# Bucket pass of a two-layer graph network: the order of sums and picks on TensorE, one-hot rows on ScalarE, index loads without bounds checks

## The reference

```python
Wh = h @ W + b
row, col = (edge_index[0], edge_index[1])     # src, dst
sc = softplus(deg_coeff[0] * deg_v + deg_coeff[1])
Wr, Wc = Wh[row], Wh[col]
dot = sum(Wr * Wc, axis=-1)
sim = dot / maximum(sqrt(sum(Wr * Wr)) * sqrt(sum(Wc * Wc)), EPS)
base = adj_v * sc * (row != col)
prop_pos = segment_sum((base * relu(sim))[:, None] * Wc, row)
prop_neg = segment_sum((base * -relu(-sim))[:, None] * Wc, row)
out = scale * (coeff[0] * prop_pos + coeff[1] * prop_neg + coeff[2] * Wh)
```

## Time and profile before

| | |
|---|---|
| median of 3 runs | 9028.44 us (9014.64 to 9034.27) |
| the profiled execution | 9029.22 us |
| its span, first to last instruction | 9027.7 us |
| mean granted TensorE clock | 0.755 |
| busy: PE, DVE | 5872.2, 4667.3 us (65%, 52%) |
| busy: ACT, POOL | 2507.0, 5394.6 us (28%, 60%) |

### The profile page before, as it was taken

One profiled execution on the slowest core, in us unless ns is written; L12 is line 12 of the kernel. 1 busy time (PEld: TensorE's weight loads), 2 busy tenths in 40 slices (PEclk: granted clock), 3 DMA queues, 4 the chain that ended last, 5 costly groups with the idle time before them and its releaser, 6 DMA issues. The chain is left out here.

```text
span 9027.7 us, 97916 instructions
## 1 busy us (share of the span) xinstructions
PE 5872.2 (65%) x22770; PEld 3836.2 (42%) x22771; DVE 4667.3 (52%) x8116; ACT 2507.0 (28%) x4153; POOL 5394.6 (60%) x5308
## 2 busy tenths in 40 slices
PE   0088888888705787777772354444444478888886
PEld 0044444444402444444441232222222268888886
DVE  2645555555433444444443454444444467777777
ACT  0044444444402444444441122222221211111111
POOL 5777777777667777777776477777777710000000
PEclk9988888888856888888886566666666667777776
DMA  9344444444423333333331122222222111111111
GB/s 340 95 127 128 132 127 132 127 132 126 137 67 84 102 102 102 101 101 103 102 101 41 41 66 64 63 63 63 64 63 63 56 45 40 41 40 39 40 41 35
DMA packets 561626, 798.11 MB, mean 88 GB/s; under 512 B 162586, under 2 KB 306858, under 8 KB 553354
## 3 DMA queue, kind: packets, MB, share of 16 engines
q1 hardware_dynamic: 371912, 482.15, 17.6%
q0 software_dynamic: 172640, 195.75, 10.3%
q10 hardware_dynamic: 16994, 119.45, 3.2%
HBM read 497.93 MB, written 298.87 MB: 88 GB/s over the span
## 5 line engine op out<-in xcount | busy, mean ns | idle before, releaser
L691 POOL DMA_INDIRECT rows_by_src_bucket<-arena,put_idx x1568 | 1604.2, 1023 | 493.9 <-issue 443.5
L623 POOL DMA_INDIRECT G<-h_rows,src_idx x1568 | 1542.6, 984 | 477.8 <-issue 477.5
L623 POOL DMA_INDIRECT G<-in_x,src_idx x1470 | 1557.3, 1059 | 448.0 <-issue 435.1
L743 PE MATMUL ps_gv<-arena,w_src 128*128 128x512 f32 x1568 | 1013.6, 783 | 0.0
L805 PE MATMUL ps_pos<-arena 128*128 128x392 f32 x390 | 325.3, 937 | 1047.4 <-DVE arena L1171 1047.4
L740 PE MATMUL ps_gv<-attr,w_attr 65*128 65x512 f32 x1568 | 1000.8, 773 | 0.0
L1209 DVE TENSOR_SCALAR arena<-ps_gv 128x512 f32<-128x512 f32 x392 | 266.7, 680 | 1279.4 <-PE ps_gv L746 1279.0
L733 PE MATMUL ps_two<-ident,G 128*128 128x128 f32 x1568 | 303.1, 326 | 762.5 <-DMA G<-h_rows,src_idx 428.1
L1150 DVE TENSOR_TENSOR_SCAN xd_t<-same,xd_t,ps_two 128x512 f32<-128x512 bf16 x588 | 749.6, 1275 | 88.6 <-PE ps_two L722 46.1
L722 PE MATMUL ps_two<-ident,inj 128*128 128x128 f32 x2352 | 399.2, 298 | 606.9 <-DMA inj<-first_edge_rows 606.9
L919 ACT COPY arena<-ps_out 128x512 f32<-128x512 f32 x392 | 229.7, 586 | 2004.9 <-PE ps_out L753 2004.9
(11 more groups left out here) (221 smaller groups left out, 10040.4 us busy)
## 6 DMA issues: line engine op xcount, KB each, us to landing
inj<-first_edge_rows SPq DMA_DIRECT2D x588, 256.0 KB, 3.0
running_sums<-arena SPq DMA_DIRECT2D x392, 256.0 KB
same<-same_dst SPq DMA_DIRECT2D x1176, 64.0 KB, 2.6
rows_by_src_bucket<-zeros ACTq DMA_DIRECT2D x62, 1072.0 KB
first_edge_rows<-zeros ACTq DMA_DIRECT2D x56, 896.0 KB, 5.8
attr<-in_attr_t SPq DMA_DIRECT2D x392, 128.0 KB, 3.6
G<-h_rows,src_idx POOLq DMA_INDIRECT x1568
rows_by_src_bucket<-arena,put_idx POOLq DMA_INDIRECT x1568, 2.3
```

The lines of the kernel that those rows point to most:

```text
L623: pool.indirect_dma_start(out_, None, table_in, bass.IndirectOffsetOnAxis(ap=index, axis=0)).then_inc(s, 16)
L691: pool.indirect_dma_start(bucket_d, bass.IndirectOffsetOnAxis(ap=put_idx[:, buf, k:k + 1], axis=0), put[:, buf, k], None).then_inc(s_added ...
L743: pe.matmul(ps_gv[:, buf % 2, k], w_src[:, layer, k], xs_t[:, buf % 2], start=False, stop=False)
```

## The change

There are three parts, and one line of set-up that goes with the second.

- On TensorE the arguments of `pipeline` are exchanged: sums of n-1 first, then picks of n, then marks of n+2.
- The one-hot rows are made by ScalarE (`make_marks`) and no longer by VectorE: the absolute value of lane minus row, with the negated row number as a per-partition bias, eight times 128x128, and then relu(1 - that) over all 1024 columns in place. The row numbers are negated where they are first computed.
- The bounds checks of the index loads on TensorE and VectorE are left out. The loads stay.

```diff
@@ pick, TensorE
-                        min_val=0, max_val=(NT - 1) * (D + 1))[1]
+                        min_val=0, max_val=(NT - 1) * (D + 1),
+                        skip_runtime_bounds_check_because="a count of bucket ends, at most NT - 1")[1]
...
@@ TensorE
-            pipeline(pe, (pick, 0), (sum_unit, 1), (turn_marks, -2), n=NU, trips=UTRIPS)
+            pipeline(pe, (sum_unit, 1), (pick, 0), (turn_marks, -2), n=NU, trips=UTRIPS)
@@ ScalarE
+            def make_marks(h, buf):
+                act.wait_ge(s_unit[buf], h * 16 + 16)
+                act.wait_ge(s_outs, udone(h, buf, NB))
+                row_now = rows[buf].rearrange("p a (j f) -> p (a j) f", f=RW)[:, :, ROW_AT]
+                for k in range(SLOTS):
+                    away = nc.scalar.activation(onehot[:, buf % NB, k], lane[:], ACT.Abs, bias=row_now[:, k:k + 1])
+                steps.then(away)
+                both = onehot[:, buf % NB].rearrange("p k e -> p (k e)")
+                nc.scalar.activation(both, both, ACT.Relu, bias=1.0, scale=-1.0).then_inc(s_onehot, 1)
...
+            steps.begin()
+            for buf in range(3):
+                make_marks(0, buf)
+            steps.end()
             copy_marks(0, 0)
-            pipeline(act, (copy_marks, -1), (roots, 0), n=NU, trips=UTRIPS)
+            pipeline(act, (copy_marks, -1), (roots, 0), (make_marks, -3), steps=steps, per=NU, n=NU, trips=UTRIPS)
@@ VectorE, set-up
-            then(v.tensor_scalar(row_of[:], deg_tmp, 0.0, None, ALU.add))
+            then(v.tensor_scalar(row_of[:], deg_tmp, -1.0, None, ALU.mult))
@@ VectorE, bucket pass
-            def mark_rows(h, buf):
-                dve.wait_ge(s_unit[buf], h * 16 + 16)
-                dve.wait_ge(s_outs, udone(h, buf, NB))
-                row_now = rows[buf].rearrange("p a (j f) -> p (a j) f", f=RW)[:, :, ROW_AT]
-                v.tensor_tensor(onehot[:, buf % NB], across(lane[:], SLOTS), along(row_now, P),
-                                ALU.is_equal).then_inc(s_onehot, 1)
...
-                        max_val=(NT - 1) * D)[1]
+                        max_val=(NT - 1) * D,
+                        skip_runtime_bounds_check_because="a count of bucket ends, at most NT - 1")[1]
...
-            for buf in range(3):
-                mark_rows(0, buf)
-            pipeline(dve, (weigh, 0), (add_unit, 2), (mark_rows, -3), steps=steps, per=8 * NU, n=NU, trips=UTRIPS)
+            pipeline(dve, (weigh, 0), (add_unit, 2), steps=steps, per=8 * NU, n=NU, trips=UTRIPS)
```

## The result

The changed kernel takes 10,147 us (median; 10,144 to 10,152) against 9,025 in runs of the kernel before on the same chip: ratio 1.1245, 95% interval 1.1225 to 1.1264. It is slower by an eighth, as forecast (10,080 in a range of 9,640 to 10,200). The profiled execution has a span of 10,150.7 us and took 10,152.3.

A forecast was written before the change was run, and what follows sets the result against it. TensorE, nearly full in the bucket pass at mixed clock, and VectorE at the high level bound the kernel. The new serial loop takes 11.05 us for 6.81: 247 periods give +1047, start +6, over 9029.2: 10,080 us, range 9,990 to 10,200.

The forecast's parts named there:

- The loop: Bucket pass: picks, weigh, add, sums, next picks run serially, 11.33 us a unit at the low clock, 7.98 at the high.
- The clock: TensorE's clock in the bucket pass: low in bursts, rising at their end; one twelfth of burst time high, 11.05 us a unit.
- all low: Edge case of the bucket pass with the clock never high in the bursts: 10,151 us.
- The earlier trace: Profile before the change: in the scatter pass the clock is low in bursts (0.53) and high just behind them (0.97).
- a rise at the end of each burst: TensorE's clock in the bucket pass rises as a burst ends, is spent in the gap, now and then reaches first sums.
- a quarter of the burst time at the high level: Bucket pass case with more of TensorE's burst time at the high clock: put at 10,000 us.
- ScalarE: One-hot rows on ScalarE: 3.4 us a unit, 0.30 per small activation, 4.6 in all, covered by the loop: zero added.
- The checks: Index loads on TensorE (0.59 us) and VectorE (0.34) stay covered without checks: zero; at most 37 and 42 us more.
- The one-hot rows and the ends: VectorE's 1.23 us a unit is worth nothing in the new loop; pass start +6 us, end 0.
- signs: Expected in the changed profile of the pass: VectorE's share near 40%, ScalarE's above 40%, clock 0.5 to 0.65.
- the sums do not hold up the picks: Rival for the bucket pass: weights ready when TensorE asks, 5.83 us a unit with today's clock mix, 8,793 us; chance 0.03.

The follow-up runs named there:

- the filled gap: Changed kernel with two unread fp32 128x384 products per unit added on TensorE behind the marks: 10,590.0 us, ratio 1.0513 to the kernel before.
- rest_alone: Changed kernel with TensorE's old order (picks of n, sums of n-1, marks of n+2): 8,490.1 us, ratio 0.9416 to the kernel before.
- pe_checks_kept: Kernel before with one-hot rows on ScalarE and VectorE's index loads unchecked, TensorE's checks and old order kept: ratio 0.9863.
- checks_alone: Kernel before with only the bounds checks of TensorE's and VectorE's index loads left out: ratio 0.9665.

## Why the prediction was right

*The loop.* It closes as written: picks, weigh, add, sums, picks. By its own terms it is 11.33 us at the low level; the timeline has 11.32 and the pass 11.34. The order alone gave 11.90 against an expected 11.85, and moving the add out gave 0.54 against 0.47.

*The clock.* This is the term that was mis-sized. I took one twelfth of the burst time at the high level (0.28 us a unit, 69 us). The clock of the pass is 0.51, so next to nothing of it reached the bursts, and the value for all low that I gave as an edge, 10,151, is what was measured; the 69 us are the distance from forecast to result (67). The earlier trace rows had the level of the bursts right. Its other half, a rise at the end of each burst which is spent in the gap, mostly did not come. Here is a microsecond inside the gap that ends at 8599.67 (length, busy us of PE, clock, DMA), and the clock stays at 0.50:

```profile
8598.00:8599.00 1.00, 0.00 (x0) 0.50 0.00 0
```

By the trace's record of the clock it was high in nine stretches of the pass, 31 us in all, and TensorE worked for 7 us of them: the high part did lie mostly in gaps, but in few of 247. Why the clock rose behind bursts of the scatter pass and seldom here stays open. That the gap in each unit keeps the clock low is shown by the filled gap (clock 0.82 and 2.5 us less) together with rest_alone. One sum beside the forecast was wrong, and nothing rests on it: a quarter of the burst time at the high level makes 11.33 - 3.35/4 = 10.49 us a unit and 9,944 us, not 10,000.

*ScalarE.* The term was zero and is zero; its root waits for VectorE in every unit, never the other way. The price was 0.30 us per small activation; these rows have it:

```profile
L998 ACT ACTIVATE arena<-arena 128x1024 f32<-128x1024 f32 x245 | 259.0, 1057 | 7.7
L1003 ACT COPY arena<-ps_gv 128x1024 f32<-128x1024 f32 x246 | 244.9, 995 | 1.1 <-PE ps_gv L831 1.1
L995 ACT ACTIVATE arena<-lane,G 128x128 f32<-128x128 f32 x744 | 226.5, 387 | 0.0
```

One takes 387 ns, and eight in a row take 2.45 us (the timeline of rest_alone has them so), 0.29 apart. The Trainium skill (ScalarE: Activation LUTs, "What ACT_TABLE_LOAD costs") gives 280 + 107 = 387 ns for one and an overlap of 93 between neighbours; the trace agrees with both. With 1.06 for the large one the marks cost 3.5 us, for which I had 3.4.

*The checks.* Their loads are covered, as forecast: the 2.55 us of idle ahead of the sums end with the add, never with a load. What I did not see is what they were worth in the old order.

*The one-hot rows and the ends.* VectorE's 1.23 us bought nothing in the serial loop: the 0.56 us a unit between the order alone (11.90) and the whole change (11.34) are the 1.17 us of idle ahead of every second add, and leave nothing for the one-hot rows. As signs I had given shares near 40% for VectorE and above 40% for ScalarE; they are 32% and 40%. The pass starts 4.9 us later, for which I had 6.

*What was right for half a reason.* The rival "the sums do not hold up the picks" was given 8,793 us. That version exists and takes 8,490. The step that failed there is the assumption that it keeps today's mix of clock levels. So the prediction sized the loss rightly against the kernel before, but against what the rest of the change could do the order costs 1,654 us of pass (1147.5 to 2801.0): 3.3 us a unit for the serial loop at the high level (7.98 against 4.65), and 3.4 for the clock. For the first I have 8.13 measured with the filler; the split rests on that.

## What to carry to other kernels

In a software pipeline on an in-order engine, write out which engine's answer each instruction waits for and what stands behind it: an operation that waits for a result of the last round must not stand ahead of the one that starts the next round. Price every change that opens or closes idle time on TensorE at both clock levels; in this pass the clock about doubled the cost of the bad order, and made the checks cost 406 us where their stalls alone are 110. When a bundle of edits is slower, run its parts: here two of the three together made the kernel 6% faster.

## What the runs showed of the hardware

- Work of 8.8 us in a row with gaps of 2.5 us left the clock at 0.51 over 2800 us. The Trainium skill (TensorE: Matmul & The Clock Gate, "Why this matters for your kernels") lets the clock fall only in a longer idle gap; the traces do not agree: it fell after a gap of 1.39 us too (the rows of pe_checks_kept) and after waits of 0.66 (the rows of checks_alone), and it stayed low through bursts that by that page should lift it.
- With no wait of TensorE above half a microsecond the same instructions ran at 1.00 for over 1000 us (rest_alone, 7300 to 8400).
- Two more fp32 products 128x384 per unit, which nobody reads, shortened a unit from 11.34 to 8.80 us.
